# Cross-attention on one core: probability units of one key tile and two heads instead of one head and two key tiles, values multiplied in two visits a group instead of three

## The chip, the core and the metric

The kernel runs on one core of one Trainium2 chip. The metric is the device time of one execution in microseconds; each kernel is run several times and the median is taken. The outputs are float32.

## What is computed

A decoder layer on 8 sequences of 224 tokens with 512 channels, 16 heads of 32, and a context of 750 tokens for each sequence. Cut to what matters here:

```
x      = layernorm(tgt) ; self-attention (causal) ; result = tgt + sa_out
xq     = layernorm(result, ln2) ;  xs = layernorm(src, ln2)
k2, v2 = split(xs @ ed_wkv) ;      q2 = xq @ ed_wq          # 16 heads of 32
wei2   = softmax(q2 k2^T * 512**-0.5)                       # 224 x 750 for each sequence and head
result = result + (wei2 v2) @ ed_wproj + ed_bproj
result = result + relu(layernorm(tgt, ln3) @ ff_w1 + ff_b1) @ ff_w2 + ff_b2
```

The change is in `wei2 v2` and in the sums that divide it.

## The kernel before

The feed-forward part runs first (to about 330 us), then self-attention with the query projection of cross-attention; cross-attention starts beside its end, at about 700 us, takes the rest and is where the change lies.

Cross-attention works on groups. A group G is four heads of one sequence: 8 sequences of 4 groups, 32 in all. The 750 keys are six tiles of 125. Every engine walks the same list, made by `plan_cross_attention`, and takes from it what is its own; each engine keeps that order, and semaphores hold it where it runs ahead. The list is cut into steps s and each step into 12 slots. Step s mixes the stages of several groups: the key projection of group s (K), the scores of group s - 1 for their row maxima ("score", 16 a group), the maxima's transpose of group s - 2 (M), the probabilities of group s - 3 ("prob", a unit in each slot) and the end of group s - 4. g = s mod 4 says what else fills the slots: value projections (V, in slots 4, 5, 8, 9 for g = 1 and 5, 6, 8, 9 for g = 2), the transposes of the next context (T, slots 4 to 11 for g = 3), and output products (E, slots 6, 7, 9, 10 for g = 0 from the third sequence on). From step 32 on there are no keys left and a few output products fill the end.

A unit u of a group is two matmuls on TensorE (line 1744) into one PSUM bank of a pair, and one exponential on ScalarE (line 1607) that writes 125 x 448 numbers to `probT`. TensorE waits for the exponential two units back. Before the change unit u has head u % 4 and the key tiles 2 (u // 4) and the next, so four units make a pair of tiles for all four heads, and `probT` is three buffers, one for each pair.

The values of a pair are multiplied in a visit ("value", line 1773): for each of the two tiles four matmuls, one for each head, that write 32 PSUM partitions each and lie side by side in the array. Pair 0 is visited in slot 7, pair 1 in slot 10, pair 2 in slot 3 of the next step, right before the sums' product with ones ("D", line 1791). The trace shows each of these float32 matmuls as two. The sums themselves ("sum") add the pair's two tiles, 125 x 896 numbers each, into `partial`: one addition for pair 0 (line 1582, in slot 3), two for each other pair (line 1586, in slots 7 and 11), on GpSimd, and in the last three groups partly on VectorE (line 1672). VectorE divides (lines 1705, 1707), ScalarE and GpSimd split the result in two halves.

VectorE reads each score's maximum out of PSUM (line 1664). The scores (line 1759) have three banks, so a score waits until the one three before it is read.

## Time and profile before

| | us |
|---|---|
| median of 3 runs | 1371.91 |
| the runs | 1371.72, 1371.91, 1375.64 |
| span of the profiled execution | 1372.2 |

The profiled execution has no time of its own beside its span; the span lies 0.3 us above the median.

| engine | busy us | share of the span |
|---|---|---|
| TensorE, matmuls | 1310.9 | 96% |
| TensorE, weight loads | 1082.5 | 79% |
| VectorE | 794.4 | 58% |
| GpSimd | 701.5 | 51% |
| ScalarE | 662.1 | 48% |

Matmuls are pipelined, and their ends are modelled, so that busy time of TensorE says that it has work and not that it is at its peak. In the timelines an instruction's duration reaches over the start of the next; starts are what to compare. The chain of waits gives each piece only what it adds to the end.

### The profile page before, as it was taken

The numbers are of one execution on the slowest core, as the hardware profiler recorded it, in microseconds if no ns is written. First come the engines' busy times: TensorE is split into PE (matmuls) and PEld (weight loads), VectorE is DVE, ScalarE is ACT, GpSimd is POOL, SyncE is SP. The second block draws the span as 40 slices with busy tenths as digits, with TensorE's granted clock in tenths as the row PEclk, the third lists the DMA queues.
The fourth block names the chain that finished last, engine by engine and source line by source line (L and its number), as shares of the span: only waits on it lengthen the run. The fifth ranks groups of instructions, "written<-read, shape, count | busy, mean of one in ns | idle before, by whom it ended". The sixth has DMA issues, their size and how long they took to land.

```text
span 1372.2 us, 24578 instructions
## 1 busy us (share of the span) xinstructions
PE 1310.9 (96%) x9193; PEld 1082.5 (79%) x9193; DVE 794.4 (58%) x2007; ACT 662.1 (48%) x1609; POOL 701.5 (51%) x577
## 2 busy tenths in 40 slices
PE   7999999999899999998788999999999999999997
PEld 6888888888788888887677787878877787887874
DVE  6613223232777777776655575756757566575565
ACT  5311111232666665666433656474665647456444
POOL 3232221322444555556733767666676766667661
PEclk9999999999999999999599999999999999999999
DMA  7400102114647776547267685777677587766641
GB/s 237 145 18 16 62 31 77 46 60 117 139 86 178 166 186 148 122 123 185 63 142 119 100 128 98 132 123 125 101 127 120 101 137 104 142 101 112 90 71 41
DMA packets 100400, 151.67 MB, mean 111 GB/s; under 512 B 10197, under 2 KB 63229, under 8 KB 99514
## 3 DMA queue, kind: packets, MB, share of 16 engines
q1 hardware_dynamic: 100282, 150.11, 53.8%
q8 instruction: 73, 1.20, 0.4%
q14 instruction: 45, 0.37, 0.1%
HBM read 66.74 MB, written 24.12 MB: 66 GB/s over the span
## 4 chain that ended last, share of the span: by engine, by line
PE 76%; POOL 8%; issue 5%; DVE 5%; DMA 3%; ACT 2%; SPq 1%; POOLq 0%; ACTq 0%; DVEq 0%
PE ps L1727 18%; PE ps L453 11%; PE ps L164 10%; PE ps L423 10%; PE ps_pair L1744 6%; PE ps L1759 5%; PE ps L1773 5%; PE ps L1832 3%; POOL ca_partial L1586 2%; DMA ca_k_stack<-ca_keys 2%; POOL ca_xT L1473 1%; DMA sa_K_stack<-sa_rows 1%; PE ps L1207 1%; PE ps L1791 1%; PE ps L1227 1%
## 5 line engine op out<-in xcount | busy, mean ns | idle before, releaser
L1664 DVE TENSOR_REDUCE ca_maxes<-ps 112x1 f32<-112x375 f32 x512 | 256.5, 541 | 106.0 <-PE ps L1759 103.9
L1607 ACT ACTIVATE ca_probT<-ps_pair 125x448 f32<-125x448 f32 x384 | 210.3, 554 | 181.5 <-PE ps_pair L1744 179.6
L1586 POOL TENSOR_TENSOR ca_partial<-ca_partial,ca_probT 125x896 f32<-125x896 f32 x118 | 249.2, 2112 | 93.6 <-ACT ca_probT L1607 89.0
L312 POOL TENSOR_TENSOR ff_hT<-ff_hrelu,ff_hT 128x512 fp32r<-128x512 f32 (+1 forms) x64 | 77.9, 1218 | 203.2 <-DVE ff_hT L394 203.2
L1759 PE MATMUL ps<-ca_k_stack,ca_q_stack 96*112 96x376 f32 x512 | 168.7, 352 | 6.9 <-issue 3.6
L1744 PEld LDWEIGHTS ps_pair<-ca_q_stack,ca_k_stack 98*125 98x125 f32 x768 | 130.2, 186 | 44.0 <-issue 31.9
L1744 PE MATMUL ps_pair<-ca_q_stack,ca_k_stack 98*125 98x224 f32 x768 | 156.2, 285 | 1.3 <-ACT ca_probT L1607 1.2
L423 PE MATMUL ps<-ff_w,ff_hT 128*128 128x512 f32 x672 | 155.5, 390 | 0.0
L1727 PE MATMUL ps<-w_b,ca_xT 128*125 128x512 f32 x576 | 151.2, 398 | 3.1 <-POOL ca_xT L1473 2.5
L1727 PE MATMUL ps<-ca_xT,w_a 128*128 128x376 f32 x768 | 153.1, 335 | 0.0
L423 PEld LDWEIGHTS ps<-ff_w,ff_hT 128*128 128x128 f32 x672 | 125.6, 188 | 25.8
L1038 ACT ACTIVATE sa_prob<-sa_prob,sa_maxes 112x112 f32<-112x112 f32 (+1 forms) x256 | 109.2, 428 | 67.0 <-DVE sa_maxes L1112 66.9
L341 ACT ACTIVATE ff_hrelu<-ps,columns 128x512 f32<-128x512 f32 (+1 forms) x64 | 40.7, 636 | 200.9 <-PE ps L453 194.5
L1727 PEld LDWEIGHTS ps<-ca_xT,w_a 128*128 128x128 f32 x768 | 130.3, 189 | 0.6
L1112 DVE CUSTOM_DVE_ANT_0 sa_prob<-ps_pair,sa_masks 112x112 f32<-112x112 f32 (+1 forms) x256 | 74.5, 328 | 87.7 <-PE ps_pair L1197 86.2
L1727 PEld LDWEIGHTS ps<-w_b,ca_xT 128*125 128x125 f32 x576 | 105.7, 188 | 23.3 <-ACT ca_xT_f L1651 3.5
L394 DVE CAST ff_hT<-ff_hrelu 128x512 fp32r<-128x512 f32 (+1 forms) x64 | 27.8, 437 | 147.0 <-ACT ff_hrelu L341 146.8
L1582 POOL TENSOR_TENSOR ca_partial<-ca_probT 125x896 f32<-125x896 f32 x32 | 67.8, 2117 | 71.6 <-PE ps L1791 39.5
L1759 PEld LDWEIGHTS ps<-ca_k_stack,ca_q_stack 96*112 96x112 f32 x512 | 86.3, 177 | 20.0 <-DVE ca_maxes L1664 10.9
L1773 PE MATMUL ps<-ca_probT,ca_v 125*32 125x224 f32 x1536 | 92.6, 359 | 0.6 <-ACT ca_probT L1607 0.6
L1713 DVE TENSOR_TENSOR ca_keys<-ps,ca_keys 128x376 fp32r<-128x376 f32 x64 | 35.2, 550 | 77.5 <-ACT ca_keys L1640 77.5
L155 POOL TENSOR_TENSOR sa_rows<-sa_f,one 128x224 fp32r<-128x224 f32 x64 | 40.3, 629 | 76.0 <-ACT sa_f L1093 61.5
(145 smaller groups left out, 2433.0 us busy)
## 6 DMA issues: line engine op xcount, KB each, us to landing
ca_k_stack<-ca_keys SPq DMA_DIRECT2D x96, 376.0 KB, 8.0
sa_Q_stack<-sa_rows SPq DMA_DIRECT2D x96, 112.0 KB, 3.5
sa_K_stack<-sa_rows SPq DMA_DIRECT2D x96, 112.0 KB, 3.7
ca_q_stack<-q_out SPq DMA_DIRECT2D x96, 112.0 KB, 9.5
ctx_tokens<-in_ctx_dram SPq DMA_DIRECT2D x14, 672.0 KB
...
```

The source lines that it names most:

```text
L164: mm = pe.matmul(acc, lhs(a, k), rhs(b, k), start=n == 0, stop=n == len(steps) - 1)
L312: pool.tensor_tensor(hT[:, LO, m % RING, 0:width(g)], hrelu[i % 2][:, 0:width(g)], hT[:, HI, m % RING, 0:width(g)].bitcast(F32), ALU.subtr ...
L423: mm = pe.matmul(ps_y[t], hT[:, a, (KT * c + k) % RING, P * t:P * (t + 1)], w2[c][:, b, k, :], start=(c, k, a, b) == (0, 0) + PASSES[0], s ...
L453: mm = pe.matmul(ps_h[i % 2][:, 0:width(g)], w1[c][:, a, k, P * (m % KT):P * (m % KT + 1)], xT[:, b, k, tokens(g)], start=(k, n) == (0, 0) ...
L1038: ins = act.activation(prob[:, n % 4, TQ * q:TQ + T * q], prob[:, n % 4, TQ * q:TQ + T * q], ACT.Exp, bias=maxes[:, n % 4, q:q + 1], scale ...
L1586: pool.tensor_tensor(total, total, half(a), ALU.add).then_inc(partial_done, 1)
L1607: act.activation(probT[u // GH][0:JT, u % GH].rearrange("p a t -> p (a t)"), ps_p[u % 2][0:JT, 0:2 * T], ACT.Exp).then_inc(exp_done, 1)
L1664: dve.tensor_reduce(maxes[:, q, j, a:a + 1], ps_s[n % 3][0:TQ, 0:JH], AX_X, ALU.max).then_inc(s_read, 1)
L1727: mm = pe.matmul(acc, lhs(a, k), rhs(b, k), start=(k, i) == (0, 0), stop=(k, i) == (3, 2))
L1744: mm = pe.matmul(ps_p[n % 2][0:JT, T * i:T * (i + 1)], k_stack[:, h, t // 3, JT * (t % 3):JT * (t % 3 + 1)], q_stack[:, h, :], start=True, ...
L1759: pe.matmul(ps_s[n % 3][0:TQ, 0:JP], q_stack[0:KS, h, TQ * q:TQ * (q + 1)], k_stack[0:KS, h, a, :], start=True, stop=True).then_inc(s_psum, 1)
L1773: mm = pe.matmul(ps_o[HD * j:HD * (j + 1), 0:T], v[b % 2][:, t, HD * h:HD * (h + 1)], probT[pair][0:JT, j, i], start=t == 0, stop=t == NT - 1)
```

## The change

A unit is now one key tile and two heads: u // 2 is the tile, 2 (u % 2) the first head. `probT` is two buffers of three tiles, laid out by tile, then head. The values are multiplied in two visits of three tiles each, 12 matmuls: the first in slot 9, the second in slot 3 of the next step. The sums are added tile by tile, each in a slot of its own (3, 5, 7, 9 and 11), the first of them tile 0 + tile 1. In the last three groups VectorE takes the tiles that stand in `VECTOR_SUMS`; in the very last, tiles 4 and 5 go to TensorE's product with ones, as the last pair did before. `partial` moves to another address, and the wait for stored results from GpSimd's first sum to ScalarE's seventh exponential.

```diff
-VECTOR_SUMS = {3: (2,), 2: (1, 2), 1: (1,)}
+VECTOR_SUMS = {3: (4, 5), 2: (2, 3, 4, 5), 1: (2, 3)}
+OWN_SUMS = (4, 5)
...
             if i == 3 and 0 <= s - 4 < NG:
-                items.append(("value", s - 4, 2))
+                items.append(("value", s - 4, 1))
...
-            if i % 4 == 3 and 0 <= s - 3 < NG and (s - 3, i) != (NG - 1, SLOTS - 1):
-                items.append(("sum", s - 3, i))
+            if i % 2 == 1 and i > 1 and 0 <= s - 3 < NG and (s - 3 < NG - 1 or i // 2 not in OWN_SUMS):
+                items.append(("sum", s - 3, i // 2))
...
-            if i in (7, 10) and 0 <= s - 3 < NG:
-                items.append(("value", s - 3, (i - 7) // 3))
+            if i == 9 and 0 <= s - 3 < NG:
+                items.append(("value", s - 3, 0))
...
-    probT = [sb(f"probT_{i}", [P, GH, 2, T], F32, offset) for i, offset in enumerate((152704, 159872, 122240))]
-    partial = sb("partial", [JT, GH, T], F32, 129408)
+    probT = [sb(f"probT_{i}", [P, HT, GH, T], F32, offset) for i, offset in enumerate((156288, 122240))]
+    partial = sb("partial", [JT, GH, T], F32, 152704)
...
+            pool.wait_ge(exp_done, UNITS * G + 2 * t + 2)
+            if t == 1:
                 if G >= 1:
                     pool.wait_ge(d_psum, G)
-                pool.tensor_tensor(total, half(0), half(1), ALU.add).then_inc(partial_done, 1)
+                pool.tensor_tensor(partial[:], tile_of(0), tile_of(1), ALU.add).then_inc(partial_done, 1)
             else:
-                for a in range(2):
-                    pool.wait_ge(partial_done, sums_of(G, pair - 1) + a)
-                    pool.tensor_tensor(total, total, half(a), ALU.add).then_inc(partial_done, 1)
+                pool.wait_ge(partial_done, SUMS * G + t - 1)
+                pool.tensor_tensor(partial[:], partial[:], tile_of(t), ALU.add).then_inc(partial_done, 1)
...
-            if u % GH == 0 and step >= PAIRS:
-                act.wait_ge(value_done, step - PAIRS + 1)
-                act.wait_ge(partial_done, sums_of(G - 1, u // GH))
+            if u % HU == 0 and G > 0:
+                act.wait_ge(value_done, HALVES * (G - 1) + half + 1)
+                act.wait_ge(partial_done, SUMS * (G - 1) + HT * half + HT - 1)
...
-            _, G, pair = item
-            b, step = G // KT, PAIRS * G + pair
-            pe.wait_ge(exp_done, GH * (step + 1))
+            _, G, half = item
+            b = G // KT
+            pe.wait_ge(exp_done, HU * (HALVES * G + half + 1))
...
-            wait_acc_read(pe, "V", b, 2 * pair + 1)
-            for i in range(2):
-                t = 2 * pair + i
+            wait_acc_read(pe, "V", b, HT * half + HT - 1)
+            for t in range(HT * half, HT * (half + 1)):
                 for j in range(GH):
                     h = GH * (G % KT) + j
                     mm = pe.matmul(ps_o[HD * j:HD * (j + 1), 0:T], v[b % 2][:, t, HD * h:HD * (h + 1)],
-                                   probT[pair][0:JT, j, i], start=t == 0, stop=t == NT - 1)
+                                   tile_of(t)[:, j], start=t == 0, stop=t == NT - 1)
```

How the order moves. On TensorE, a step with g = 1, from the last score of slot 9 to the first key projection of the next step (`ca_k_stack,ca_q_stack` into `ps_pair` is a unit, into `ps` a score; `ca_probT,ca_v` is a visit). Before:

```order
L1759 MATMUL ps<-ca_k_stack,ca_q_stack 112x376
L1744 MATMUL ps_pair<-ca_q_stack,ca_k_stack 125x224 x2
L1759 MATMUL ps<-ca_k_stack,ca_q_stack 112x376 x2
L1773 MATMUL ps<-ca_probT_113,ca_v_111 32x224 x8
L1744 MATMUL ps_pair<-ca_q_stack,ca_k_stack 125x224 x2
L1759 MATMUL ps<-ca_k_stack,ca_q_stack 112x376 x2
L1744 MATMUL ps_pair<-ca_q_stack,ca_k_stack 125x224 x2
L1727 MATMUL ps<-ca_xT,w_a 128x376 x6
```

And now:

```order
L1761 MATMUL ps<-ca_k_stack,ca_q_stack 112x376
L1774 MATMUL ps<-ca_probT_112,ca_v_111 32x224 x12
L1746 MATMUL ps_pair<-ca_q_stack,ca_k_stack 125x224 x2
L1761 MATMUL ps<-ca_k_stack,ca_q_stack 112x376 x2
L1746 MATMUL ps_pair<-ca_q_stack,ca_k_stack 125x224 x2
L1761 MATMUL ps<-ca_k_stack,ca_q_stack 112x376 x2
L1746 MATMUL ps_pair<-ca_q_stack,ca_k_stack 125x224 x2
L1729 MATMUL ps<-ca_xT,w_a 128x376 x6
```

The visit of slot 10 is gone and one of 12 stands ahead of the unit of slot 10, so two units and four scores follow each other.

On TensorE, a step with g = 0 and output products (`ca_wp`, `wp_lo`), from the last score of slot 7 to the first output product of slot 9. Before:

```order
L1759 MATMUL ps<-ca_k_stack,ca_q_stack 112x376
L1773 MATMUL ps<-ca_probT_112,ca_v_111 32x224 x8
L1744 MATMUL ps_pair<-ca_q_stack,ca_k_stack 125x224 x2
L1759 MATMUL ps<-ca_k_stack,ca_q_stack 112x376 x2
L1744 MATMUL ps_pair<-ca_q_stack,ca_k_stack 125x224 x2
L1759 MATMUL ps<-ca_k_stack,ca_q_stack 112x376
L1832 MATMUL ps<-ca_wp_103,ca_oT_120 112x512
```

And now:

```order
L1761 MATMUL ps<-ca_k_stack,ca_q_stack 112x376
L1746 MATMUL ps_pair<-ca_q_stack,ca_k_stack 125x224 x2
L1761 MATMUL ps<-ca_k_stack,ca_q_stack 112x376 x2
L1746 MATMUL ps_pair<-ca_q_stack,ca_k_stack 125x224 x2
L1761 MATMUL ps<-ca_k_stack,ca_q_stack 112x376
L1833 MATMUL ps<-ca_wp_103,ca_oT_119 112x512
```

The visit of slot 7 is gone, with nothing in its place before slot 9's end.

On GpSimd, a step with g = 3 (`ca_xT` is the low half of a transposed context tile, `ca_oT` that of a result, `ca_partial` a sum). Before:

```order
L1582 TENSOR_TENSOR ca_partial<-ca_probT_112 125x896
L1473 TENSOR_TENSOR ca_xT<-ca_xT_f_106,ca_xT 128x375 x2
L1468 TENSOR_TENSOR ca_oT_123<-ca_oT_f_3_128,ca_oT_123 128x224
L1473 TENSOR_TENSOR ca_xT<-ca_xT_f_106,ca_xT 128x375
L1586 TENSOR_TENSOR ca_partial<-ca_partial,ca_probT_113 125x896 x2
L1473 TENSOR_TENSOR ca_xT<-ca_xT_f_106,ca_xT 128x375 x4
L1586 TENSOR_TENSOR ca_partial<-ca_partial,ca_probT_114 125x896 x2
L1473 TENSOR_TENSOR ca_xT<-ca_xT_f_106,ca_xT 128x375
```

And now:

```order
L1583 TENSOR_TENSOR ca_partial<-ca_probT_112 125x896
L1475 TENSOR_TENSOR ca_xT<-ca_xT_f_106,ca_xT 128x375
L1586 TENSOR_TENSOR ca_partial<-ca_partial,ca_probT_112 125x896
L1475 TENSOR_TENSOR ca_xT<-ca_xT_f_106,ca_xT 128x375
L1470 TENSOR_TENSOR ca_oT_122<-ca_oT_f_3_127,ca_oT_122 128x224
L1475 TENSOR_TENSOR ca_xT<-ca_xT_f_106,ca_xT 128x375
L1586 TENSOR_TENSOR ca_partial<-ca_partial,ca_probT_113 125x896
L1475 TENSOR_TENSOR ca_xT<-ca_xT_f_106,ca_xT 128x375 x2
L1586 TENSOR_TENSOR ca_partial<-ca_partial,ca_probT_113 125x896
L1475 TENSOR_TENSOR ca_xT<-ca_xT_f_106,ca_xT 128x375 x2
L1586 TENSOR_TENSOR ca_partial<-ca_partial,ca_probT_113 125x896
L1475 TENSOR_TENSOR ca_xT<-ca_xT_f_106,ca_xT 128x375
```

The sum of tile 2 has moved ahead, behind the first low half; three sums stand ahead of the fourth low half, as before, and the same number in all.

## Rows read from the trace of the kernel before

**Rows 1.** Windows by stage, one batch of cross-attention: us, busy time (instructions), clock, DMA.
```profile
1071.00:1148.00 77.00, 75.86 (x571) 60.99 (x570) 48.82 (x101) 44.61 (x89) 51.91 (x33) 1.00 0.75 125
```

**Rows 2.** Waits of weight loads in cross-attention: total us, times, longest.
```profile
PEld ps_pair L1744 <- issue: 31.9, 89, 0.4
PEld ps L1773 <- issue: 19.6, 81, 0.3
...
PEld ps L1759 <- DVE ca_maxes L1664: 5.6, 17, 0.9
```

**Rows 3.** Chain of waits, 1111 to 1173 us: start, us on the chain, what.
```profile
1111.84 0.89 PE ps L1773 x16
1112.73 0.38 PE ps L1791 x8
1113.11 0.41 PE ps_pair L1744 x2
...
1117.23 0.21 PE ps_pair L1744 x2
...
1172.86 0.43 PE ps L1791 x8
```

**Rows 4.** Timelines, step of the last keys, TensorE then VectorE: start, us, instruction.
```profile
1319.48 0.48 PE L1744 MATMUL ps_pair<-ca_q_stack,ca_k_stack 98*125 98x224 f32 x2
...
1320.36 0.84 PE L1759 MATMUL ps<-ca_k_stack,ca_q_stack 96*112 96x376 f32 x2
1321.04 0.38 PE L1744 MATMUL ps_pair<-ca_q_stack,ca_k_stack 98*125 98x224 f32 x2
...
1323.60 0.38 PE L1744 MATMUL ps_pair<-ca_q_stack,ca_k_stack 98*125 98x224 f32 x2
...
1320.17 2.82 DVE L1664 TENSOR_REDUCE ca_maxes<-ps 112x1 f32<-112x375 f32 x6 [0.64 <-PE ps L1759]
```

**Rows 5.** Timelines, slot 7 of a step with output products, TensorE then VectorE.
```profile
1099.07 0.33 PE L1759 MATMUL ps<-ca_k_stack,ca_q_stack 96*112 96x376 f32 x1
...
1099.27 0.69 DVE L1721 TENSOR_TENSOR ca_res<-ps,ca_res 112x512 f32<-112x512 f32 x1 [0.79 <-PE ps L1832]
1099.88 0.54 DVE L1664 TENSOR_REDUCE ca_maxes<-ps 112x1 f32<-112x375 f32 x1
```

**Rows 6.** Timelines, step with transposes of the context, TensorE, ScalarE, GpSimd.
```profile
1160.89 0.54 PE L1819 MATMUL ps<-ident,ctx_tokens 125*128 125x125 f32 x3 [0.29 <-ACT ca_xT_f L1651]
...
1162.43 0.54 PE L1819 MATMUL ps<-ident,ctx_tokens 125*128 125x125 f32 x3 [0.45 <-ACT ca_xT_f L1651]
...
1163.07 0.96 PE L1773 MATMUL ps<-ca_probT,ca_v 125*32 125x224 f32 x16
...
1164.45 0.48 PE L1819 MATMUL ps<-ident,ctx_tokens 125*128 125x125 f32 x3
...
1165.67 1.63 PE L1727 MATMUL ps<-w_b,ca_xT 128*125 128x512 f32 x6 [0.35 <-POOL ca_xT L1473]
...
1155.10 0.54 ACT L1607 ACTIVATE ca_probT<-ps_pair 125x448 f32<-125x448 f32 x1
...
1164.13 0.77 ACT L1648 ACTIVATE ca_xT<-ps,columns 128x375 fp32r<-128x375 f32 x1
...
1155.28 0.99 POOL L1473 TENSOR_TENSOR ca_xT<-ca_xT_f,ca_xT 128x375 fp32r<-128x375 f32 x1 [1.34 <-ACT ca_xT_f L1651]
...
1158.49 0.66 POOL L1468 TENSOR_TENSOR ca_oT<-ca_oT_f,ca_oT 128x224 fp32r<-128x224 f32 x1
...
1160.31 4.28 POOL L1586 TENSOR_TENSOR ca_partial<-ca_partial,ca_probT 125x896 f32<-125x896 f32 x2
```

**Rows 7.** Waits of ScalarE in cross-attention.
```profile
ACT ca_keys L1640 <- DMA ca_k_stack<-ca_keys: 3.7, 1, 3.7
```

**Rows 8.** Timelines, end of cross-attention, TensorE then ScalarE.
```profile
1342.18 0.59 PE L1791 MATMUL ps<-ca_partial,ca_ones 125*32 125x224 f32 x8
...
1359.46 0.54 ACT L1607 ACTIVATE ca_probT<-ps_pair 125x448 f32<-125x448 f32 x1 [0.76 <-PE ps_pair L1744]
```

More of the change, by code:

```diff
@@ L1606, in scalar @@
                 act.wait_ge(what, n * B)
-            act.activation(probT[u // GH][0:JT, u % GH].rearrange("p a t -> p (a t)"),
+            if (G, u) == (0, HU):
+                what, n = sa.done["results_stored"]
+                act.wait_ge(what, n * B)
+            t, heads = unit(u)
+            act.activation(tile_of(t)[:, heads].rearrange("p j t -> p (j t)"),
                            ps_p[u % 2][0:JT, 0:2 * T], ACT.Exp).then_inc(exp_done, 1)
@@ L1666, in vector @@
         if name == "sum" and by_vector(*item[1:]):
[L1667 to L1672 removed]
+            _, G, t = item
+            dve.wait_ge(exp_done, UNITS * G + 2 * t + 2)
+            dve.wait_ge(partial_done, SUMS * G + t - 1)
+            dve.tensor_tensor(partial[:], partial[:], tile_of(t), ALU.add).then_inc(partial_done, 1)
         if name == "negate":
@@ L1733, in tensor @@
             _, G, u = item
-            n, h, pair = UNITS * G + u, GH * (G % KT) + u % GH, u // GH
+            n, (t, heads) = UNITS * G + u, unit(u)
             if n == 0:
@@ L1742, in tensor @@
             for i in range(2):
-                t = 2 * pair + i
+                h = GH * (G % KT) + heads.start + i
                 mm = pe.matmul(ps_p[n % 2][0:JT, T * i:T * (i + 1)],
@@ L1785, in tensor @@
             G = item[1]
-            own = range(2) if G == KT * B - 1 else ()
+            own = OWN_SUMS if G == KT * B - 1 else ()
             pe.wait_ge(partial_done, SUMS * (G + 1) - len(own))
             for j in range(GH):
-                terms = [partial[:, j]] + [probT[PAIRS - 1][0:JT, j, i] for i in own]
+                terms = [partial[:, j]] + [tile_of(t)[:, j] for t in own]
                 for n, term in enumerate(terms):
```

33 lines of the change are left out of this document (11 added, 22 removed).

## The prediction

> **What bounds the kernel now.** I read in this order: the page, the windows by stage, what the weight loads and the other engines waited for, the chain of waits, and then the timelines of single steps. The window of a batch in the middle shows TensorE with 75.86 of 77 us busy at full clock (1.00, its 2.4 GHz level), the other engines at 40 to 70% [rows 1]. That says that it always has a matmul in flight, not that each is as short as it can be. The waits of the weight loads show what is left [rows 2]: 51.5 us of "issue" around the visits to the values, and 5.6 us behind VectorE's maxima, though VectorE is idle a third of the time. So the end of cross-attention is set by TensorE's order of work, by its transitions, and in places by an engine that it has run ahead of. The question for each matmul that goes is what stands next in line there.
>
> **The visit and its price.** The chain shows a visit of 8 value matmuls (16 in the trace, four heads side by side, so 4 rounds) at 0.89 us; the sums behind it, 8 in the trace and 2 rounds, take 0.38 us, 0.19 a round [rows 3]. So 0.13 us of a visit (0.89 less 4 x 0.19) is entry. The unit behind a visit takes 0.41 us where one elsewhere takes 0.21 [rows 3]: 0.20 us is exit. The Trainium skill, "TensorEngine Tiling (Array Packing)", Key Properties, says that a change of tiling mode drains TensorE. By that rule alone every visit saved is time saved, in all 32 groups; the rows agree that there is a price, and what it buys is the first rival.
>
> A visit of 12 was not run before. I put it at 0.13 + 6 x 0.19 = 1.27 us; its bounds are 1.34 (one and a half visits of 0.89) and 1.14 (no entry). In slots 7 to 10 a group then loses 2 x (0.89 + 0.20) = 2.18 and gains 1.27 + 0.20 = 1.47: 0.71 us less. In slot 3 the last visit grows by two rounds: 0.38 us more. Net 0.33 us less TensorE work a group, if nothing comes in its place. Something does, and where depends on what the visit covered.
>
> **Steps with projections in slots 8 and 9 (14 groups).** Scores go through three PSUM banks, so each waits until VectorE has read the third before it. Now two units and four scores follow each other in slots 10 and 11 with no visit between. The trace has this very run once before: in the step of the last keys, behind a visit, unit, two scores, unit, two scores. The first unit starts at 1319.48 and the next after the run at 1321.04, 1.56 us; VectorE's six maxima behind it take 2.82 us [rows 4]. Without a wait the same run takes 1.22 (by starts in that timeline 0.32 from the first unit to its score, 0.17 from a score to what follows it, four times, and 0.22 from the second unit to its score). The wait is 0.34 us. -0.71 + 0.34 + 0.38 = +0.01, times 14: +0.1. Bounds for the wait: 0 and 0.54 (next paragraph), -4.6 to +2.9 for all.
>
> **Steps with two output products (6 groups).** The score before the visit in slot 7 starts at 1099.07; VectorE first adds a result (1099.27, 0.69) and reads the score from 1099.88 to 1100.42 [rows 5]. The visit hid that. Without it the fourth operation behind that score, the first score of slot 9 (its bank is that of the score named), is due at 1099.07 + 0.17 + 0.22 + 0.17 + 0.17 + 0.22 = 1100.02 and gets its bank at about 1100.46, and a weight load that has waited costs 0.10 more (0.27 to the next start instead of 0.17 [rows 4]): 0.54. -0.71 + 0.54 + 0.38 = +0.21, times 6: +1.3. Bounds 0 and 0.71 for the wait: -2.0 to +2.3.
>
> **Steps that transpose the next context (7 groups).** Here ScalarE goes without a pause: transposes of slot 10 start at 1162.43, when ScalarE has let go of the bank, then comes the visit (1163.07), the last transposes at 1164.45, and the values' projection at 1165.67, behind a GpSimd queue of two sums and a low half [rows 6]. With the visit one slot earlier: transposes of slot 9 at 1160.89 as before (ScalarE), the visit 0.64 later as behind slot 10 now, 1161.53, unit 1162.80, transposes 1163.29 (0.49 behind a unit that carries an exit: 1163.07 + 0.89 = 1163.96, and they start at 1164.45), the last ones 0.88 later at 1164.17 (0.49 to the unit, then 0.22 and 0.17 for a unit and a score; the bank is free by 1163.9, for ScalarE ends an exponential behind that copy before 1164.13), unit 0.49 later, projection 0.22 later: 1164.88, 0.79 us earlier. ScalarE reads the slot 10 transposes from 1164.13; they are ready at 1163.29 + 0.54 = 1163.83, so it does not stop. GpSimd must be ready too. One sum moves ahead between its first and second low half. From 1155.28 it does 0.99, 2.14 (the sum; its exponentials end at 1155.64), 0.99, 0.66, 0.99, 2.14 and 0.99 in a row, no input late: 1164.2, before 1164.88 [rows 6]. So -0.79 + 0.38, and 0.05 that the group sums lose to GpSimd behind this step (0.43 for 0.38 [rows 3]) goes: -0.46, times 7: -3.2. Bounds: nothing gained but the 0.38 paid, +2.7, and the full gain of slots 7 to 10 and more, 1.09, -5.3.
>
> **The rest.** The step of group 1: ScalarE stands 3.7 us for the key transfer one step later [rows 7], so what slots 7 to 10 give is lost, and 0.38 stays. The step of group 28 (last keys, slots 6 to 11 paced by maxima): its slots end at 1323.60 [rows 4]; the maxima's queue without the visit in slot 7 lets them end no more than 0.13 sooner, by my count of its reads; +0.25. Group 29: VectorE has the last two sums, one now in slot 9, 1.1 us; this pushes the maxima as far back as the missing visit had brought them forward; the value visit before the group sums has two more rounds, and they start 0.4 later than 1342.18 [rows 8]: +0.4. Group 30: paced by exponentials of 0.55 in a row, the visit in slot 9 waits for nothing: 0 (-0.5 to +0.4). Group 31: two visits less and a longer one bring the unit of slot 11 forward, but its exponential now waits for slot 10's: they end at about 1360.3 instead of 1360.0 [rows 8], and the last visit, with everything behind it, is 0.38 longer: +0.7.
>
> What costs nothing: the sums stay five a group, 896 columns, 2.1 us on GpSimd and 1.1 on VectorE, now read in one piece; no row shows a strided read to be slower or faster, and GpSimd has the 0.7 us above to spare. Exponentials stay twelve of 448 columns, units two matmuls. Buffers: ScalarE's first write to a half waits for a visit in slot 9 and a sum of slot 5, both 2 slots past; of the second half, for slot 3. The wait for the stored results moves from GpSimd's first sum to ScalarE's seventh exponential; the first sum waits for an exponential in the trace, not for that transfer, and it stood earlier in the order. No DMA is added or moved.
>
> **Sum**: +0.1 + 1.3 - 3.2 + 0.4 + 0.25 + 0.4 + 0 + 0.7 = -0.05 us. The profiled span is 1372.2; the median of the runs is 1371.9, 0.3 below it. Forecast: 1371.8, the median as good as unmoved. The work that goes was cover.
>
> **Rivals.**
> 1. *Faster: the drains are bought for real.* The waits for maxima don't come, since VectorE starts its reads sooner than I let it. For: 51.5 us of issue waits around visits [rows 2], and TensorE is busy 98.5% [rows 1]. Against: rows 4 show the very run with its wait. By the drain rule of the Trainium skill's tiling page it comes to the same as here. Price: 32 x 0.33 = 10.6, 1361.3 us. It decides where the average wait is under 0.2 us.
> 2. *Slower: rounds go from covered places into an uncovered one.* Slot 3 has projections before it and the group sums behind it, nothing to hide 0.38 us, while waits in slots 7 to 11 eat all of the 0.71. For: the two cases above eat 0.34 and 0.54. Price: 32 x 0.38 = 12.2, less 7 x 0.79 in the transposing steps, +6.7: 1378.6 us. It decides from an average wait of 0.6.
> 3. *Slower: the sum moved ahead holds up GpSimd's low halves*, so that the projection waits as long as now and the transposing steps only pay 0.38. +3.2 + 2.7 = +5.9, 1377.7 us. For: that queue is on the chain. Against: the total ahead of the half is the same, and it starts sooner.
> 4. *The change does less than it says*: that the two visits are one in the order is seen in the rows of the order, so this has no chance of its own.
>
> **Chances.** Forecast 0.60, with its own range 1368 to 1375.5; rival 1 0.24 (all its cases from a third of the price up); rival 2 0.10; rival 3 0.06. About 0.3%, 4.1 us, is what a measurement of this kernel tells from no change. Faster by more: 0.24 and the forecast's lower edge, 0.26; slower by more: 0.16 less what of the rivals stays small, 0.14; within: 0.60. The range goes from 1365 (it leaves out the better half of rival 1) to 1376.5 (it leaves out most of rivals 2 and 3).
>
> **What would show it.** Visits of 24 in the chain at 1.27 us, 64 of them; issue waits of the weight loads down by a third, some 34 us. Weight loads of scores behind the maxima up from 5.6 us (with 17 waits) to 10 or more, with some 20 new ones, in slot 11 and at the start of slot 9. The projection behind the transposes at 0.8 us earlier against ScalarE's last transpose copy, its GpSimd releaser gone. Last exponential to end 0.4 us longer. If the waits for maxima stay near 6 us, rival 1 is right; if the waits for maxima pass 15 us and the end is later by more than 4 us, rival 2; if a low half still releases the projection, rival 3.

## The result and the profile after

| | before | after |
|---|---|---|
| median, us | 1372.66 (4 runs) | 1380.33 (4 runs) |
| lowest to highest | 1371.72 to 1375.64 | 1378.84 to 1382.01 |
| span of the profiled execution | 1372.2 | 1379.9 |

The change makes the kernel slower: the ratio is 1.0056 (95% interval 1.0042 to 1.0070). The forecast was 1371.8 with a range from 1365 to 1376.5; the time lies above it, 1.7 us above the price of rival 2.

What answers to [rows 2], the waits of the weight loads in cross-attention, with two kinds that were smaller before, 5.2 and 3.5 us (total us, times, longest):

```profile
PEld ps_pair L1746 <- issue: 23.2, 64, 0.7
PEld ps L1761 <- DVE ca_maxes L1668: 15.2, 40, 1.4
PEld ps L1774 <- issue: 13.3, 49, 0.3
...
PEld ps_pair L1746 <- ACT ca_probT L1611: 8.7, 19, 0.9
PEld ps L1729 <- ACT ca_xT_f L1655: 4.6, 7, 0.7
```

The issue waits fall from 51.5 to 36.5 us, so transitions really went. The waits for maxima grow from 5.6 to 15.2, those of units for exponentials to 8.7 and those of projections for ScalarE's copies to 4.6. The stretch that answers to [rows 1] (us, then busy time of TensorE, its weight loads, VectorE, ScalarE, GpSimd, granted clock, DMA share, GB/s):

```profile
1073.00:1150.00 77.00, 74.94 (x559) 60.96 (x558) 48.10 (x101) 44.42 (x89) 53.08 (x33) 1.00 0.75 125
```

TensorE has 74.94 of 77 us of work where it had 75.86. It does less, and finishes later.

**Where the time went.** The best ruler is the start of the group sums' product with ones ("D"), which ends a group. TensorE's timeline has these starts in one batch after the change:

```profile
1093.63 0.56 PE L1792 MATMUL ps<-ca_partial,ca_ones 125*32 125x224 f32 x8
...
1114.47 0.56 PE L1792 MATMUL ps<-ca_partial,ca_ones 125*32 125x224 f32 x8
...
1134.22 0.56 PE L1792 MATMUL ps<-ca_partial,ca_ones 125*32 125x224 f32 x8
...
1153.56 0.56 PE L1792 MATMUL ps<-ca_partial,ca_ones 125*32 125x224 f32 x8
...
1175.43 0.56 PE L1792 MATMUL ps<-ca_partial,ca_ones 125*32 125x224 f32 x8
```

Their distances are 20.84, 19.75, 19.34 and 21.87 us, for a g = 0, 1, 2 and 3 step (from its slot 3 to the next step's, so each holds all visits of one group), and they repeat from batch to batch within 0.1. Before they were 20.75, 19.67, 18.86 and 21.62. So a batch is 0.9 us longer: +0.09, +0.08, +0.48, +0.25. Up to group 28's sums that makes 5.6 (+0.74 in the first four distances, five times +0.90, +0.32 in the four before the end). The last three distances, from group 28's sums to 31's, take 36.94 instead of 32.18, +4.8. The first sums stand 1.6 earlier and what follows the last sums is 1.0 shorter; both lie almost wholly in code that the change leaves alone, the latter since the clock was 0.66 there before (1365 to 1370 us) and 1.00 after. 5.6 + 4.8 - 1.6 - 1.0 = 7.8, the growth of the span within 0.1.

**The g = 0 step**, against [rows 5]: TensorE's timeline around the first score of slot 9.

```profile
1100.79 0.34 PE L1761 MATMUL ps<-ca_k_stack,ca_q_stack 96*112 96x376 f32 x1
1100.97 0.38 PE L1746 MATMUL ps_pair<-ca_q_stack,ca_k_stack 98*125 98x224 f32 x2
1101.18 0.51 PE L1761 MATMUL ps<-ca_k_stack,ca_q_stack 96*112 96x376 f32 x2
1101.53 0.38 PE L1746 MATMUL ps_pair<-ca_q_stack,ca_k_stack 98*125 98x224 f32 x2
1102.19 0.43 PE L1761 MATMUL ps<-ca_k_stack,ca_q_stack 96*112 96x376 f32 x1 [0.28 <-DVE ca_maxes L1668]
1102.45 0.39 PE L1833 MATMUL ps<-ca_wp,ca_oT 128*112 128x512 f32 x1
```

The score of 1102.19 was due 0.22 behind the unit, at 1101.75; it starts 0.44 late, and the next matmul follows 0.26 behind it instead of 0.17. That is 0.53 us, the 0.54 of the forecast.

**The g = 2 step.** TensorE's timeline, slots 7 to 11:

```profile
1138.93 0.38 PE L1746 MATMUL ps_pair<-ca_q_stack,ca_k_stack 98*125 98x224 f32 x2
1139.15 0.51 PE L1761 MATMUL ps<-ca_k_stack,ca_q_stack 96*112 96x376 f32 x2
1139.84 0.48 PE L1746 MATMUL ps_pair<-ca_q_stack,ca_k_stack 98*125 98x224 f32 x2 [0.19 <-ACT ca_probT L1611]
...
1143.94 1.34 PE L1774 MATMUL ps<-ca_probT,ca_v 125*32 125x224 f32 x24
1145.21 0.48 PE L1746 MATMUL ps_pair<-ca_q_stack,ca_k_stack 98*125 98x224 f32 x2
...
1146.77 0.38 PE L1746 MATMUL ps_pair<-ca_q_stack,ca_k_stack 98*125 98x224 f32 x2
```

and ScalarE beside it:

```profile
1138.28 0.37 ACT L1632 CAST ca_oT<-ca_oT_f 128x224 fp32r<-128x224 f32 x1
1138.55 0.82 ACT L1617 ACTIVATE ctx_tokens<-ctx_tokens,ca_shift,ctx_ln_rstd 125x512 f32<-125x512 f32 x1
1139.27 0.52 ACT L1611 ACTIVATE ca_probT<-ps_pair 125x448 f32<-125x448 f32 x1
```

The visit of 12 takes 1.27 us (1143.94 to 1145.21), and the run of two units and four scores behind it 1.56 (1145.21 to 1146.77), both as forecast. What the forecast lacks stands before them: the unit of slot 8 (1139.84) waits for the exponential of slot 6, which stands in ScalarE's queue behind a rounding of a result and a normalisation. The scores ahead of it are through by 1139.50 (1139.15 and twice 0.17), so the wait is 0.34, and its first score follows at 0.32 instead of 0.22. In the kernel before, the visit in slot 7 stood exactly there.

**The g = 3 step**, against [rows 6]: TensorE's last transposes and the projection, then ScalarE's copies.

```profile
1164.03 1.34 PE L1774 MATMUL ps<-ca_probT,ca_v 125*32 125x224 f32 x24
...
1166.69 0.48 PE L1820 MATMUL ps<-ident,ctx_tokens 125*128 125x125 f32 x3
...
1168.03 1.67 PE L1729 MATMUL ps<-w_b,ca_xT 128*125 128x512 f32 x6 [0.47 <-ACT ca_xT_f L1655]
```

```profile
1165.67 0.76 ACT L1655 ACTIVATE ca_xT_f<-ps,columns 128x375 f32<-128x375 f32 x1
...
1167.19 0.79 ACT L1655 ACTIVATE ca_xT_f<-ps,columns 128x375 f32<-128x375 f32 x1
```

GpSimd no longer releases the projection, as forecast. But ScalarE does: the projection takes the bank of the transposes of slot 10, and the copy that empties it ends at 1167.98. ScalarE works without a pause, one transposed tile every 1.52 us (1165.67 to 1167.19). The projection starts 14.47 us behind the sums (1168.03 less 1153.56) instead of 14.60, and slot 3 then costs 0.38 more.

**The end.** In the step that ends with group 29's sums, VectorE, GpSimd and TensorE:

```profile
1336.51 1.45 DVE L1470 TENSOR_TENSOR ca_oT<-ca_oT_f,ca_oT 128x224 fp32r<-128x224 f32 x1
...
1335.62 4.32 POOL L1586 TENSOR_TENSOR ca_partial<-ca_partial,ca_probT 125x896 f32<-125x896 f32 x2
...
1338.47 0.56 PE L1761 MATMUL ps<-ca_k_stack,ca_q_stack 96*112 96x376 f32 x1 [1.18 <-DVE ca_maxes L1668]
```

A subtraction of VectorE takes 1.45, beside GpSimd's sum, and ends at 1337.96, just behind the first of the two sums (1335.62 + 2.10 = 1337.72). In the kernel before it had no sum beside it:

```profile
1332.56 0.38 DVE L1468 TENSOR_TENSOR ca_oT<-ca_oT_f,ca_oT 128x224 fp32r<-128x224 f32 x1
```

The maxima queue behind it, TensorE stands 1.18 us, and then its clock is at the low level, 1.2 GHz: 0.53 granted on average from 1338.4 to 1342, where before it was 1.00 all through:

```profile
1338.40:1342.00 3.60, 3.52 (x11) 2.91 (x12) 2.48 (x6) 0.54 (x1) 1.54 (x1) 0.53 0.00 0
```

This step is 2.76 us longer. In the next two (+0.47 and +1.53) units stand up to 0.74 for exponentials, behind ScalarE's rounding of the result, and the last visit 0.85 instead of 0.63.

### The profile page after: what moved, and what is told of

It reads as the page before. It is cut to its first block, busy times and chain, and to the rows that moved or that the text cites. A ratio compares the mean times of both kernels' runs of the same rounds, so it can differ in the third digit from the quotient of the medians.

```text
span 1379.9 us, 24579 instructions
## 1 busy us (share of the span) xinstructions
PE 1306.3 (95%) x9193; PEld 1084.8 (79%) x9193; DVE 794.1 (58%) x2007; ACT 663.3 (48%) x1609; POOL 701.0 (51%) x577
## 4 chain that ended last, share of the span: by engine, by line
PE 69%; ACT 7%; DVE 7%; issue 6%; POOL 5%; DMA 4%; SPq 1%; POOLq 0%; ACTq 0%; DVEq 0%
PE ps L1729 17%; PE ps L453 11%; PE ps L423 10%; PE ps L164 8%; PE ps L1774 5%; PE ps_pair L1746 5%; PE ps L1761 4%; PE ps L1833 3%; DMA ca_k_stack<-ca_keys 2%; ACT ca_xT_f L1655 2%; ACT ca_probT L1611 2%; ACT ca_xT L1652 2%; DMA sa_K_stack<-sa_rows 1%; DVE ca_maxes L1668 1%; PE ps L1792 1%
## 5 line engine op out<-in xcount | busy, mean ns | idle before, releaser
L1761 PE MATMUL ps<-ca_k_stack,ca_q_stack 96*112 96x376 f32 x512 | 174.5, 358 | 12.5 <-DVE ca_maxes L1668 5.5
L1774 PE MATMUL ps<-ca_probT,ca_v 125*32 125x224 f32 x1536 | 85.9, 357 | 0.8 <-ACT ca_probT L1611 0.8
L1715 DVE TENSOR_TENSOR ca_keys<-ps,ca_keys 128x376 fp32r<-128x376 f32 x64 | 35.1, 549 | 75.4 <-ACT ca_keys L1644 75.4
```

What stands on the lines that cost most here:

```text
L1761: pe.matmul(ps_s[n % 3][0:TQ, 0:JP], q_stack[0:KS, h, TQ * q:TQ * (q + 1)], k_stack[0:KS, h, a, :], start=True, stop=True).then_inc(s_psum, 1)
L1774: mm = pe.matmul(ps_o[HD * j:HD * (j + 1), 0:T], v[b % 2][:, t, HD * h:HD * (h + 1)], tile_of(t)[:, j], start=t == 0, stop=t == NT - 1)
```

## The experiments

Each kernel was timed beside the kernel before on the same chip. The steps are the better ruler: the first group sums, with little of any edit ahead of them, start anywhere from 767.2 to 775.8 us in these profiled executions, and that moves a whole time by more than most steps do. The four numbers on the right are the distances of the group sums in the steady batches (two values where they alternate), then their sum, and the span from group 28's sums to group 31's.

| kernel | median us | ratio to before, 95% | g = 0, 1, 2, 3 | batch | end |
|---|---|---|---|---|---|
| before | | | 20.75, 19.67, 18.86, 21.62 | 80.9 | 32.2 |
| the change | 1380.3 | 1.0056 (1.0042-1.0070) | 20.84, 19.75, 19.34, 21.87 | 81.8 | 36.9 |
| e1 three visits | 1370.5 | 0.9995 (0.9984-1.0005) | 20.65, 19.60/.65, 18.92, 21.47 | 80.7 | 33.6 |
| e2 low half on GpSimd | 1377.5 | 1.0041 (1.0027-1.0056) | 20.84, 19.67/.75, 19.35, 21.87 | 81.8 | 34.1 |
| e3 visit in slot 7 | 1383.3 | 1.0086 (1.0072-1.0100) | 20.30, 20.31, 19.42, 21.85 | 81.9 | 35.0 |
| e4 = e1 + e2 | 1371.0 | 0.9996 (0.9986-1.0006) | 20.64, 19.61/.68, 18.92, 21.47 | 80.7 | 33.2 |
| e5 four tiles, two | 1375.2 | 1.0023 (1.0009-1.0036) | 20.84, 19.44, 19.00, 21.78 | 81.1 | 35.1 |
| e6 visit in slot 10 | 1374.2 | 1.0024 (1.0015-1.0032) | 20.83, 19.32/.41, 19.00, 21.85 | 81.0 | 35.3 |
| e7 half maxima | 1377.7 | 1.0044 (1.0030-1.0057) | 20.64, 19.47, 19.14, 21.84 | 81.1 | 36.5 |
| e8 = e1 + e7 | 1371.6 | 0.9996 (0.9984-1.0008) | 20.65, 19.34/.42, 18.92, 21.46 | 80.4 | 33.0 |
| e9 visits by step | 1366.0 | 0.9960 (0.9948-0.9973) | 20.31, 19.33, 18.89, 21.47 | 80.0 | 33.6 |
| e10 half copies | 1374.3 | 1.0020 (1.0010-1.0031) | 20.84, 19.75, 19.35, 20.93 | 80.9 | 37.0 |
| e11 = e1 + e10 | 1364.9 | 0.9954 (0.9940-0.9968) | 20.65, 19.60, 18.92, 20.54 | 79.7 | 33.6 |
| e12 side work later | 1380.1 | 1.0068 (1.0053-1.0083) | 20.84, 19.75, 19.02, 21.88 | 81.5 | 37.1 |
| e13 = e7 + e12 | 1370.6 | 0.9996 (0.9985-1.0006) | 20.64, 19.15, 18.69, 21.85 | 80.3 | 33.4 |
| e14 e9, g = 2 too | 1366.7 | 0.9960 (0.9944-0.9976) | 20.31, 19.33/.41, 18.67, 21.49 | 79.8 | 36.3 |
| e15 e14, its end as e9 | 1366.3 | 0.9962 (0.9948-0.9976) | 20.30, 19.41, 18.67, 21.49 | 79.9 | 34.7 |

### Three visits, and the end: e1 to e4

e1 keeps the new units, buffers and sums, and puts the visits back to two tiles each, in slots 7, 10 and 3:

```diff
-                items.append(("value", s - 4, 1))
+                items.append(("value", s - 4, 2))
...
-            if i == 9 and 0 <= s - 3 < NG:
-                items.append(("value", s - 3, 0))
+            if i in (7, 10) and 0 <= s - 3 < NG:
+                items.append(("value", s - 3, (i - 7) // 3))
...
```

> The changed kernel with its new units and sums, but three visits as before: tiles 0 and 1 in slot 7, 2 and 3 in slot 10, 4 and 5 in slot 3. Theory A (the moved visits uncover waits that they hid): the steps between the group sums go back to those of before (19.35 to about 18.86 us in the step before the transposes, 21.87 to 21.6 in the one with them), and only what the new sums do at the end stays, about 2.8 us of group 29 less what the last products gain: 1373 to 1375.5 us. Rival B (the new units or the tile-by-tile sums cost the time, through GpSimd or ScalarE): it stays within 2 us of the changed kernel, 1378 or more.

The time is back at before's, even under what was expected: a ratio of 0.9995 where the change has 1.0056, from the visits alone. Units and sums are not the cause. By step they move 20.75, 19.67, 18.86 and 21.62 to 20.65, 19.63, 18.92 and 21.47, so they even give 0.10 in g = 0 and 0.15 in g = 3, and at the end they cost 1.4. The visits also bring back their own price: the issue waits of the weight loads are 50.5 us in e1 (31.9 and 18.6), and the waits for maxima 6.7. e2 is the change with the low half of group 28 given to GpSimd, so that VectorE does not do it beside a sum:

```diff
-        if name == "D_low" and item[1] < NG - KT:
+        if name == "D_low" and item[1] <= NG - KT:
...
```

> The changed kernel, with group 28's low half computed by GpSimd instead of VectorE. Theory A: in the changed kernel that VectorE operation took 1.45 us where it took 0.38 before, beside a GpSimd sum, TensorE then stood 1.2 us for maxima and its granted clock fell to 0.53 for 3.6 us. Without the meeting the step of group 29 (16.28 us between group sums) falls to 13.7 to 14.2, and the time by 1.5 to 3 us. Rival B (the first half of VectorE's sums in slot 9 is what is late): the step stays over 15.5 us and the time within 0.5.

The time came as expected, and the step gave more than expected: group 29's falls from 16.28 to 13.36, with 13.7 to 14.2 expected, and the clock stays at 1.00 there.

```profile
1337.00:1345.00 8.00, 7.48 (x84) 4.92 (x82) 6.58 (x13) 4.08 (x9) 2.07 (x1) 1.00 0.01 2
```

e3 is the change with the first visit in slot 7, and e4 is e1 with e2's edit.

> The changed kernel with its first visit in slot 7 instead of 9; tiles 0 to 2 are ready there. Theory A (slot 7 is where cover is missing: maxima behind the added result for g = 0, exponentials behind the context's normalisation for g = 2, the exponential behind the result's rounding in the last groups): steps with g = 2 fall by about 0.45, with g = 0 by 0.5, those with g = 1 rise by 0.1 (a longer run of scores in slots 9 to 11), the last two groups fall by 1 to 2 us together; in all 5 to 8 us less than the changed kernel, 1372 to 1375. Rival B (the two rounds in slot 3 are what costs, wherever the other visit stands): within 2 us of the changed kernel.

> Both: three visits, and group 28's low half on GpSimd. Theory A: 1 to 3 us below the run with three visits alone, 1370.5 to 1373, within 0.2% of the kernel before. Rival B: over 1375.

e4 lies within its range, but the 1 to 3 us that it was to gain on e1 did not come: 1371.0 against 1370.5, and 33.2 against 33.6 at the end. In e1 the same subtraction takes 1.45 beside a sum too, yet group 29's step is 14.35 there, 14.02 in e4, and the clock is 1.00 in both: with three visits the meeting costs 0.3, with two it costs 2.9. e3 missed: a visit in slot 7 should have given the cover back, and the kernel came out above the change. The steps show why it gained nothing. g = 0 did improve, to 20.30, the lowest of any run so far. But g = 1 rose by 0.6: without a visit in slot 10 the scores of slots 9, 10 and 11 are one run, TensorE's timeline in that step:

```profile
1045.35 0.34 PE L1761 MATMUL ps<-ca_k_stack,ca_q_stack 96*112 96x376 f32 x1
1045.53 0.38 PE L1746 MATMUL ps_pair<-ca_q_stack,ca_k_stack 98*125 98x224 f32 x2
1045.74 0.51 PE L1761 MATMUL ps<-ca_k_stack,ca_q_stack 96*112 96x376 f32 x2
1046.10 0.38 PE L1746 MATMUL ps_pair<-ca_q_stack,ca_k_stack 98*125 98x224 f32 x2
1046.33 0.43 PE L1761 MATMUL ps<-ca_k_stack,ca_q_stack 96*112 96x376 f32 x1
1047.38 0.43 PE L1761 MATMUL ps<-ca_k_stack,ca_q_stack 96*112 96x376 f32 x1 [0.62 <-DVE ca_maxes L1668]
```

Cover is needed at two places, slot 7 or 8 and slot 10, and a single visit can stand in one. That e3's median is 3 us above the change's is not explained by its steps: in the profiled executions it takes 598.0 us from the first group sums to the last, the change 599.7.

### Where the rounds stand: e5, e6

e5 multiplies tiles 0 to 3 in slot 10 and tiles 4 and 5 in slot 3; e6 is the change with its first visit in slot 10.

```diff
-            if i == 9 and 0 <= s - 3 < NG:
+            if i == 10 and 0 <= s - 3 < NG:
...
+    CUT = (0, 4, NT)
...
-            for t in range(HT * half, HT * (half + 1)):
+            for t in range(CUT[half], CUT[half + 1]):
```

> Two visits as in the change, but of unequal size: tiles 0 to 3 in slot 10, tiles 4 and 5 in slot 3. Measured so far, from group sums to group sums, in the steady batches (g = 0, 1, 2, 3, then their sum): before 20.75, 19.67, 18.86, 21.62 (80.9); the change 20.84, 19.75, 19.34, 21.87 (81.8); the change's units and sums with three visits 20.65, 19.65, 18.92, 21.47 (80.7). Theory A (the two rounds moved into slot 3 are paid in full in every step, what left slots 7 to 10 was mostly cover): slot 3 is 0.38 shorter than in the change, and a visit of 1.65 in slot 10 stands again between the two runs of scores: 20.4 to 20.65, 19.3 to 19.5, 18.9 to 19.1, 21.47; batch 80.1 to 80.7, time 1367 to 1372. Rival (two visits are in themselves the trouble, because a long one leaves ScalarE without units): the batch stays at 81.5 or more, time 1376 to 1381.

> The change with its first visit in slot 10 instead of 9, still three tiles and three tiles. Theory A: the visit parts the scores of slot 10 from those of slot 11, so the g = 1 and g = 2 steps get shorter (19.75 to 19.4-19.6, 19.34 to 19.0-19.2), the g = 3 step stays at 21.87 because its 0.38 in slot 3 is the whole difference there, g = 0 within 0.2 of 20.84. Batch 81.1 to 81.5, time 1375 to 1379. Rival (the place in slots 7 to 10 does not matter, the size in slot 3 alone does): 81.8, time as the change, 1380.

e6 came as forecast in all four steps, or up to 0.1 below, and its time 1 us below the range. e5 missed: its batch is that of e6, at 81.1 instead of 80.1 to 80.7. Two rounds moved from slot 3 to slot 10 gain at most 0.07 in any step. So slot 3 is no special place: a round costs 0.19 wherever TensorE is not waiting for another engine, in slot 10 as well. What slots 7 to 10 had was a wait to stand in, and that is the part of theory A that remains. And in g = 1 the visit that goes already pays here, with nothing else cured: 19.33 to 19.41 against the 19.60 to 19.65 of e1.

### Take the waits away: e7, e8, e12, e13

e7 is the change with VectorE's maxima over half the columns, the other half left out, and e8 the same with three visits:

```diff
-            dve.tensor_reduce(maxes[:, q, j, a:a + 1], ps_s[n % 3][0:TQ, 0:JH],
+            dve.tensor_reduce(maxes[:, q, j, a:a + 1], ps_s[n % 3][0:TQ, 0:JH // 2],
```

> The change, with VectorE's maxima taken over the first half of the columns only (the second half of each score tile is left out of the maximum): this takes the waits of TensorE for the maxima away and leaves its work as it is. Theory A (those waits ate part of what two visits give): the g = 1 step falls by 0.2 to 0.35 (19.75 to 19.4-19.55), g = 0 by 0.2 to 0.5 (20.84 to 20.35-20.65), g = 2 by 0.2 to 0.35 (19.34 to 19.0-19.15), g = 3 (no maxima in its slots 8 to 11 to wait for, ScalarE sets it) stays at 21.8-21.9. Rival (the maxima are not what is waited for): no step moves by more than 0.1. The last steps, paced by maxima, get shorter in any case, so the whole time says little: 1365 to 1377.

> The same half maxima (second half of the columns left out) in the kernel with the change's units and sums and three visits. Theory A: in the middle it did not wait for maxima, so its steps stay at 20.65, 19.65, 18.92, 21.47, within 0.05; the kernel with two visits and half maxima is then shorter than this one in the g = 1 step, by 0.1 to 0.33, and longer in the g = 3 step by 0.4. Rival (maxima pace both): its g = 1 and g = 2 steps fall as much as those of the kernel with two visits. Time 1362 to 1370.

e7 is as expected in all four steps. Both times are above their ranges, by 0.7 and 1.6 us; in the profiled executions the first sums, which have little of the edit ahead of them, stand at 773.1 and 775.8 where the change has 769.9. e8's steps are not as expected: its g = 1 step fell too, by 0.24, so two visits are still no shorter than three there (19.47 to 19.40). What is left, by theory A of the next run, is the wait for the exponential. e12 moves ScalarE's side work out of its way:

```diff
-NORMALISE = (4, 5, 6, 7, 9, 10)
+NORMALISE = (7, 7, 8, 8, 9, 10)
...
-            for j, name in enumerate(("D", "", "D_high", "D_low") if s <= NG else ("D", "D_high", "D_low")):
+            for j, name in enumerate(("D", "", "", "", "D_high", "D_low") if s <= NG else ("D", "D_high", "D_low")):
```

> The change, with ScalarE's side work moved out of slots 4 to 6: the rounding of a result from slot 5 to slot 7 (its low half from 6 to 8), the context's normalisations from slots 4, 5, 6, 7, 9, 10 to 7, 7, 8, 8, 9, 10. Nothing is left out. Theory A (with no visit in slot 7, the unit of slot 8 waits for the exponential of slot 6, which stands behind that side work): the wait goes; g = 1 from 19.75 to 19.45-19.6, g = 2 from 19.34 to 18.95-19.2, g = 0 from 20.84 by 0 to 0.2, g = 3 at 21.87 within 0.1. Time 1375 to 1379. Rival (that wait is of no account, or comes back at once in slots 10 and 11): no step moves by more than 0.1, time 1379.5 to 1382.

In g = 2, where the wait was found, it gives 0.32 as expected; in g = 1 it gives nothing, and the time, 1380.1, is above its range. In g = 1 neither cure alone reached the 19.33 of e6. e13 has both at once:

> The change with both cures at once: the half maxima (second half of the columns left out of the maximum) and ScalarE's side work moved out of slots 4 to 6. Alone, the first brought the g = 1 step from 19.75 to 19.46 and g = 2 from 19.34 to 19.14, the second left g = 1 and brought g = 2 to 19.02. Theory A (two engines are late one behind the other at slot 8; with neither late the visit that went pays its 0.33 at last): g = 1 at 19.05 to 19.25, so 0.15 to 0.35 less than the 19.40 of three visits with half maxima; g = 2 at 18.6 to 18.85, less than the 18.92 of three visits; g = 3 at 21.85. Rival (the drains of a visit are not worth their price even with nobody late): g = 1 at 19.35 or more, g = 2 at 18.9 or more. Time 1371 to 1376.

Both steps land in the range of theory A: g = 1 at 19.15 and g = 2 at 18.69, below the 19.40 and 18.92 of three visits; the time, 1370.6, is 0.4 under its range. In TensorE's timeline of g = 1 the unit of slot 8 now follows without a pause for ScalarE:

```profile
1033.94 0.38 PE L1746 MATMUL ps_pair<-ca_q_stack,ca_k_stack 98*125 98x224 f32 x2
1034.15 0.65 PE L1761 MATMUL ps<-ca_k_stack,ca_q_stack 96*112 96x376 f32 x2
1034.64 0.37 PE L1746 MATMUL ps_pair<-ca_q_stack,ca_k_stack 98*125 98x224 f32 x2
```

So for a visit in slot 9 the third visit's transitions are worth about 0.25, near the 0.33 of the forecast, once two other engines are in time. In g = 1 each had hidden the other: moving ScalarE's side work alone gives nothing, behind the shorter maxima it gives 0.3. The kernel with three visits was not run with the side work moved, so that 0.25 compares kernels that differ in this too.

### ScalarE in the transposing step: e10, e11

e10 is the change, e11 the kernel with three visits, both with a shorter first copy of each transposed tile; the second half of its columns is left out from the second sequence on:

```diff
-            act.activation(xT[:, HI, m, a, 0:JH], acc[:, 0:JH], ACT.Identity,
+            n = JH if b == 0 else JH // 2
+            act.activation(xT[:, HI, m, a, 0:n], acc[:, 0:n], ACT.Identity,
```

> The change, with ScalarE's rounded copy of a transposed context tile over the first half of its columns only, from the second sequence on (the second half keeps the first sequence's numbers): eight ScalarE operations of the g = 3 step get shorter, TensorE's work stays. Theory A (that step is set by ScalarE, which lets the projection start at 14.47 us behind the group sums with two visits as with three, so only slot 3's 0.38 is left of the change): g = 3 falls from 21.87 by 0.6 to 1.5; g = 0, 1, 2 stay within 0.05 of 20.84, 19.75, 19.34. Rival (the number or the size of the visits sets it, not ScalarE): g = 3 stays within 0.2 of 21.87. Time 1371 to 1377 by A.

> The same half copies (second half of the columns left at the first sequence's numbers) with three visits. By theory A its g = 3 step falls from 21.47 too, but by less than that of the kernel with two visits, since now TensorE's own work counts and the second visit's transitions are in the open: the difference between the two, 0.40 with whole copies, shrinks to between -0.1 and 0.2. Rival: the difference stays at 0.35 to 0.45. Time 1364 to 1370.

The g = 3 step falls by 0.94 in e10 and by 0.93 in e11, and no other step moves. ScalarE sets it. That the difference between the two would shrink was wrong: it stays at 0.39. In both the copy that empties the bank ends 13.48 us behind the sums instead of 14.42, and the projection starts at 13.53 instead of 14.47. In e11 TensorE's own work ahead of the projection ends just there, so the cut was barely too small to put TensorE last. Without it, in e1 too, ScalarE's copy releases the projection, at the same 14.47 us behind the sums as in the change (sums at 1066.36):

```profile
1080.83 1.42 PE L1730 MATMUL ps<-w_b,ca_xT 128*125 128x512 f32 x5 [0.20 <-ACT ca_xT_f L1656]
```

### The version that the runs point to: e9, e14, e15

e9 gives each step the visits that were shortest in it, by a table in place of the fixed slots:

```diff
+TWO, THREE = {0: ((7, 0, 3), (3, 3, 6)), 1: ((10, 0, 3), (3, 3, 6))}, ((7, 0, 2), (10, 2, 4), (3, 4, 6))
...
+def visits_of(G):
+
+    return TWO.get((G + 3) % 4, THREE) if 0 <= G < 28 else THREE
...
-            if i == 9 and 0 <= s - 3 < NG:
-                items.append(("value", s - 3, 0))
+            for n, visit in enumerate(visits_of(s - 3)[:-1] if 0 <= s - 3 < NG else ()):
+                if i == visit[0]:
+                    items.append(("value", s - 3, n))
...
```

> The version that the runs so far point to: each step gets the visits that were shortest in it. Groups whose units lie in a g = 0 step: tiles 0 to 2 in slot 7, 3 to 5 in slot 3; in a g = 1 step: tiles 0 to 2 in slot 10, 3 to 5 in slot 3; in g = 2 and g = 3 steps and from group 28 on: three visits of two tiles, in slots 7, 10 and 3. Theory A (a visit that goes is worth its transitions only where no engine is late behind it): the steps come out as measured one by one, 20.30, 19.33-19.41, 18.92, 21.47, the batch at 80.0 to 80.15 (before 80.9), time 1366 to 1369. Rival (the steps' gains don't add, since work pushed out of one step is late in the next): batch 80.5 or more, time 1370 or more.

The steps come out as measured one by one, the batch at exactly 80.0, and the median is 1366.0, as expected: 0.4% below the kernel before (ratio 0.9960, 0.9948 to 0.9973), which the change is 0.56% above. e14 takes g = 2 into the table too, with the side work of e12 moved and e2's edit; e15 leaves the rounding where it was in the last steps.

> The version with visits chosen by step, and the g = 2 step also with two visits (tiles 0 to 2 in slot 10, 3 to 5 in slot 3), now that ScalarE's side work is moved out of its slots 4 to 6; group 28's low half on GpSimd. Nothing is left out. Theory A: the g = 2 step, 18.89 with three visits, 19.00 with two and the side work in place, comes to 18.6 to 18.8; the others stay at 20.31, 19.33, 21.47; batch 79.75 to 79.9; time 0.5 to 2 below the 1366.0 of the version before it: 1364 to 1365.5. Rival (in g = 2 the visit in slot 7 stays needed): 18.9 or more, time 1366 or more.

> The kernel before this one (visits by step, two in the g = 2 step too, ScalarE's side work later), with the rounding of results moved only in steps that still have keys, so that the steps at the end are those of the version with side work in place. That kernel lost 2.2 us in the step of group 29, where the granted clock fell to 0.50-0.55 for some 6 us behind a stretch with TensorE busy 3.13 of 4 us. Theory A (the middle's gain is real and the loss was the clock's fall behind a wait at the end, set off by the later rounding): batch 79.8, groups 28 to 31 in 33.2 to 34, no stretch of low clock before the last output products, time 1363.5 to 1365.5. Rival (the clock falls there in any case, or in as many runs as before): time 1366 to 1367.5.

In the middle both do what was expected: g = 2 at 18.67, the batch 0.13 to 0.2 shorter. The time doesn't follow, 1366.7 and 1366.3, and both miss. The ends eat it: 36.3 and 34.7 against 33.6. In e14 the clock falls to half in a stretch in which TensorE was busy 3.13 of 4 us, and stays there:

```profile
1330.00:1334.00 4.00, 3.13 (x27) 1.95 (x27) 3.31 (x7) 2.55 (x6) 0.00 (x0) 0.85 0.01 4
1334.00:1336.00 2.00, 2.00 (x15) 1.04 (x12) 0.21 (x1) 0.54 (x1) 0.10 (x1) 0.50 0.19 56
1336.00:1340.00 4.00, 4.00 (x20) 3.07 (x23) 3.13 (x4) 1.61 (x4) 2.00 (x1) 0.55 0.49 139
```

e9 has the same gap at the same place and keeps 1.00 behind it:

```profile
1330.00:1334.00 4.00, 3.10 (x34) 2.16 (x37) 3.36 (x7) 2.60 (x6) 0.00 (x0) 1.00 0.00 0
1334.00:1340.00 6.00, 5.71 (x60) 3.63 (x59) 4.92 (x6) 3.87 (x8) 2.13 (x1) 1.00 0.41 126
```

In e15's profiled execution the clock falls at the same place again, for a shorter time:

```profile
1330.00:1334.00 4.00, 3.22 (x30) 2.04 (x28) 3.90 (x8) 1.57 (x4) 0.04 (x1) 1.00 0.02 4
1334.00:1338.00 4.00, 3.88 (x32) 1.98 (x32) 1.71 (x4) 2.24 (x6) 0.00 (x0) 0.64 0.01 2
```

So the order of the roundings is not what decides it; what decides whether a gap of this size at the end costs the clock stays open, and with it which of the three is best. e15's runs spread from 1362.8 to 1370.5, e9's from 1364.2 to 1366.3.

## Why the prediction was wrong, point by point

- **The visit and its price**: right. 1.27 us for 12, 0.38 more in slot 3. e9 shows what the third visit is worth where no new wait takes its place: 20.31 against 20.65 in g = 0 and 19.33 against 19.60 to 19.65 in g = 1, 0.34 and 0.3, for the 0.33 that was worked out. The Trainium skill, "TensorEngine Tiling (Array Packing)", Key Properties, lets a change of tiling mode drain TensorE; the traces agree, in that 15 us of issue waits go with the third visit and come back with it in e1 (50.5 us). Rival 1, by which that alone would decide, falls: the change is slower.
- **What the new units and sums do**, put at nothing but 0.05 in the transposing steps and the terms of the end: e1 shows -0.10, -0.04, +0.06 and -0.15 in g = 0 to 3, and +1.4 at the end. The change in the steps below is visits and these together.
- **Steps with projections in slots 8 and 9**, forecast +0.01 each. In g = 1 measured +0.08, near enough; the wait of the run in slots 10 and 11 is the 0.34 foretold. In g = 2 measured +0.48. The step of the prediction that failed here is "-0.71 + 0.34 + 0.38": it counts the scores' wait and no other. The unit of slot 8 waits 0.34 for ScalarE and 0.10 more for its restart. I had asked of the missing visit only what it covered on VectorE's side, and never laid ScalarE's queue beside slot 7. This is 0.47 in six steps and 0.13 in the last one, 3.0 us.
- **Steps with two output products**, forecast +0.21: measured +0.09. The wait is there at 0.53, as forecast, and against e1 with its three visits the step is 0.19 longer (20.65 to 20.84), so the mechanism and its price were right. The rest, 0.10, is what units and sums give in this step.
- **Steps that transpose the next context**, forecast -0.46: measured +0.25, 0.71 in each of the six such steps behind the first sums, 4.3 us, the largest miss. The step that failed is "unit 0.49 later, projection 0.22 later: 1164.88". For the last transposes I had checked when their bank comes free, for the projection only GpSimd. The transposes did come earlier, 13.13 instead of 13.37 us behind the sums, but in the kernel before the projection's bank was free only at 1165.46, 0.2 us ahead of its start at 1165.67 (ScalarE's copies stand 1.52 apart): behind the releaser in the trace stood another, almost as late. The 0.13 by which the projection does come earlier is in e1 too, so the visits gave nothing ahead of it and their 0.38 in slot 3 is paid in full: 21.47 to 21.87. e10 and e11 show that ScalarE sets the step with two visits and with three.
- **The rest**. Group 1, forecast +0.4: measured -0.05 (16.72 to 16.67); no run shows why. Group 28 measured +0.02 against 0.25. Group 29, forecast +0.4: measured +2.76. I had put VectorE's low half at its 0.38, and e2 shows that its place beside a GpSimd sum, and the clock behind the wait, cost 2.9 in a kernel with two visits. Group 30 +0.47 against 0, group 31 +1.53 against 0.7: ScalarE's rounding ahead of exponentials again.
- **Rivals**. Rival 2 had the sign and, at 1378.6, nearly the size, though that is partly luck: its price credits 5.5 us to the transposing steps, where the visits gained nothing, and lacks the 4.8 of the end. The waits ate 0.56 of a group's 0.71 on average (+0.90 a batch is +0.23 a group, and 0.38 - 0.71 + 0.56 = 0.23), just under the 0.6 from which it was to decide; against e1 it is 0.62, just over. Its reason, slot 3 as the uncovered place, is not the whole: e5 shows slot 10 to be no better. I had priced the waits on VectorE and missed those on ScalarE. Rival 3 falls: GpSimd no longer releases the projection.
- **What would show it**. The mark for rival 2, waits for maxima above 15 us and an end later by more than 4, was met (15.2 and 7.7). Visits at 1.27 and the GpSimd releaser gone, right; the projection 0.8 earlier, wrong (0.13); issue waits down by 15 us, not 34.
